# Filling the slots in 128 pieces, and nine part rows per lane by one repeated-source DMA

## The chip, the cores and the metric

The kernel runs on one NeuronCore of one Trainium2 chip. The metric is device time in microseconds (us) of one execution. Engines are called as in the profile: PE (matrix multiplies; PEld its weight loads), DVE, ACT, POOL, and SP, which here only issues DMAs and waits. PEq, SPq and so on are the engines' instruction queues.

## The reference

The reference is two transformer-like layers on x of 8 sequences, 512 positions, 256 channels, each sublayer followed by a residual sum and a layer norm. What matters here is the first sublayer, a state space scan:

```
def step(h, inp):
    u_t, dt_t, B_t, C_t = inp
    dA = jnp.exp(dt_t[:, :, None] * A_mean)
    dB = dt_t[:, :, None] * B_t[:, None, :]
    h = dA * h + dB * u_t[:, :, None]
    y_t = jnp.einsum('bds,bs->bd', h, C_t)
```

h is 512 channels by 128 states for each of 8 sequences, over 512 positions. Then come a gated norm and projection, a ternary feed-forward of hidden width 1024, a second mixer with cumulative sums, and a mixture of 8 experts with the top 2 of each token.

## The kernel before

The kernel has three phases. `project_phase` computes, per sequence, the inputs of the scan and writes them to DRAM. The product v = dt * u and B are written as three bf16 parts each (`v_parts`, `b_parts`), whose sum is the float32 value; dt goes out as float32 (`dt_rows`) and, for 128 of 512 channels, as three parts (`dt_parts`).

`stream_phase` is the scan, with the dense layers of the previous chunk mixed in. Positions are cut into 8 chunks of 64. A step k is one position of one half of the batch (four sequences, called lanes), so a chunk has 128 steps. In a step:
- SP loads a decay tile (`dt_rows`, L577): the dt of four lanes and 384 channels, 6 KB, repeated over 128 partitions, 768 KB in all. A ring of RING = 4 slots holds them; the slot of step k + 4 is loaded once POOL has done step k (the wait at L575).
- ACT takes the exponential of the decay tile (L1130), and of a PSUM bank for the other 128 channels (L1135), three steps ahead.
- POOL multiplies the state h by the decay tile, in two instructions (L1384); DVE does it for the other channels (L1410).
- PE forms the outer product of v and B for each lane (`x_outer`, L729): a matmul over nine rows, all pairs of the three parts of v with the three of B. DVE adds it to h (L1420).
- PE reads y out of h with C (`contract`, L755).

The nine rows of a lane come from DRAM by SP (`row_block`, L555 to L571). A row block covers four positions, that is eight steps, and is double buffered. For each of 8 lanes and each part i of B, one DMA brings the three part rows of v (three partitions of 4 KB, L568) and one brings part i of B repeated on three partitions (of 1 KB, L570): six DMAs per lane, 48 per block. PE waits for a group of four lanes at L723 and L725, on counts made from LANE_IN. The first block is issued before anything else of the scan (L683), then the four first decay tiles (L684).

SP issues everything in the order that `body` (L663) writes out: at each step the decay tile of step k + 4; then, at k % 8 = 2, 3, 4 and 5, the rows of two lanes of the next block; then the rest. In chunks 1 to 7 the rest includes weights of the dense layers (28 loads of 512 KB per chunk, L614), whose steps come from tables such as H1_AT and DONE_AT. PE, ACT and DVE have their own written-out orders: the mixer layers, norms and gate stand in about the first 50 steps of a chunk, and the two 1024 x 1024 layers in steps 50 to 113. Chunk 0 has no mixed work; chunk 1 has no second mixer; chunks 2 to 6 are five turns of a hardware loop, whose addresses are computed in registers; chunk 7 is written out.

The slot fill writes a DRAM tensor `slots` of 24 x 512 rows of 1 KB, which the last phase gathers tokens into, with valid numbers, so that unused slots hold some. It is 16 DMAs from DRAM to DRAM of 768 KB, at k = 30 and 94 of each chunk (L672). Only the end of the phase waits for them (L709).

`expert_phase` routes the tokens and runs the experts.

Of the kernel before, what the change touches and what calls it, by code (L numbers as in the profile page):

```python
# [29 lines left out]
BATCH, SEQ, DIM = 8, 512, 256  # L30
INNER = 512
STATE = 128
# [7 lines left out]
PARTS = 3  # L40
PAIRS = PARTS * PARTS
# [14 lines left out]
JOBS = 2 * BATCH + EXPERTS  # L56
# [9 lines left out]
def hold(eng, passed):  # L66

    eng.sem_inc(passed, 1)
# [323 lines left out]
LANES = 4  # L392
HALVES = BATCH // LANES
# [4 lines left out]
CHUNKS = SEQ // CHUNK  # L398
HALF_STEPS = HALVES * CHUNK
SLOTS = GROUPS * CHUNK  # L400
STEPS = 4
ROW_BLOCKS = CHUNK // STEPS
# [52 lines left out]
def stream_phase(nc, bank, d, used):  # L455
# [9 lines left out]
    with ExitStack() as ctx:  # L465
        def sb(name, shape, dt=F32):
            return ctx.enter_context(nc.sbuf_tensor(name, shape, dt))

        def sem(name):
            used.append(nc.alloc_semaphore(name))  # L470
            return used[-1]
# [4 lines left out]
        vrow = sb("s_vrow", [P, BUFS, HALVES, STEPS * INNER], BF16)  # L476
        brow = sb("s_brow", [P, BUFS, HALVES, STEPS * STATE], BF16)
# [39 lines left out]
        in_v = [[sem(f"s_in_v{r}{f}") for f in range(HALVES)] for r in range(BUFS)]  # L517
        in_b = [[sem(f"s_in_b{r}{f}") for f in range(HALVES)] for r in range(BUFS)]
# [12 lines left out]
        filled = sem("s_filled")  # L531
# [16 lines left out]
            return sems[name + str(m)]  # L548

        block = ctx.enter_context(nc.Block())  # L550
        LANE_IN = LANES * PARTS * 16

        @block.sync
        def _(sp):
            def row_block(j, buf, lanes):  # L555

                if 0 in lanes:
                    sp.wait_ge(x_ps, (j + 1) * (GROUPS * STEPS))
                    hold(sp, sp_passed)
                    sp.wait_ge(e_ps, (j + 1) * (HALVES * STEPS))  # L560
                    hold(sp, sp_passed)
                    for hf in range(HALVES):
                        sp.dma_start(drow[32 * hf:32 * hf + PARTS, buf], d["DTD_STEPS"][hf, j]
                                     ).then_inc(in_e[buf], 16)
                for s in lanes:
                    q, hf = 32 * (s % LANES), s // LANES
                    for i in range(PARTS):
                        sp.dma_start(vrow[q + PARTS * i:q + PARTS * (i + 1), buf, hf], d["V_STEPS"][s, :, j]  # L568
                                     ).then_inc(in_v[buf][hf], 16)
                        sp.dma_start(brow[q + PARTS * i:q + PARTS * (i + 1), buf, hf],  # L570
                                     d["B_STEPS"][s, i, j].partition_broadcast(PARTS)).then_inc(in_b[buf][hf], 16)  # L571

            def dt_rows(k, slot):

                sp.wait_ge(pool_kept, 2 * k + 2)  # L575
                hold(sp, sp_passed)
                sp.dma_start(decay[:, slot].rearrange("p l d -> p (l d)"), d["DTP_HALF"][k].partition_broadcast(P)  # L577
                             ).then_inc(in_dt[slot], 16)

            def c_cols(c):  # L580
                sp.wait_ge(diag_ok, c * (2 * CHUNK // DIAG))
                hold(sp, sp_passed)
                sp.dma_start(ccol[:], d["C_CHUNK"][c]).then_inc(c_in, 16)
# [58 lines left out]
            def stored(m):  # L642
                sp.wait_ge(S("out_dma"), 16 * (m + 1))
                sp.sem_inc(S("out_ok"), 1)
# [18 lines left out]
            def body(c, m, last):  # L663
                for k in range(HALF_STEPS):
                    if not (last and k + RING >= HALF_STEPS):
                        dt_rows(c * HALF_STEPS + k + RING, k % RING)
                    j, r = (k - 2) // (HALVES * STEPS) + 1, (k - 2) % (HALVES * STEPS)
                    if k >= 2 and r < 4 and not (last and j == ROW_BLOCKS):
                        row_block(c * ROW_BLOCKS + j, j % BUFS, (2 * r, 2 * r + 1))
                    if k == 104 and not last:  # L670
                        c_cols(c + 1)
                    if k % (HALF_STEPS // 2) == 30:  # L672
                        sp.dma_start(d["SLOTS_FILL"][c * 2 + k // (HALF_STEPS // 2)], d["x_rows"]).then_inc(filled, 16)
                    if m is not None:
                        first = isinstance(m, int) and m == 0
                        mix(m, k, SHORT if first else FULL, not first)
# [4 lines left out]
            sp.dma_start(a_log[:], d["A_log"]).then_inc(w_in, 16)  # L681
            sp.dma_start(ccol[:], d["C_CHUNK"][0]).then_inc(c_in, 16)
            row_block(0, 0, range(BATCH))  # L683
            for k in range(RING):  # L684
                dt_rows(k, k)
# [4 lines left out]
            chunk_xT(0)  # L690
            chunk_x(0)
            body(0, None, False)
            body(1, 0, False)
            with sp.Fori(2, CHUNKS - 1) as c:
                body(c, c - 1, False)
# [10 lines left out]
                weights(CHUNKS, LATE[i], (end, FULL[i - WRING]))  # L706
            store(end)
            stored(end)
            sp.wait_ge(filled, 16 * 2 * CHUNKS)  # L709

        @block.tensor
        def _(pe):
# [5 lines left out]
            def x_outer(c, n):  # L718
# [3 lines left out]
                if at == 0 and g % 2 == 0:  # L722
                    pe.wait_ge(in_v[buf][hf], (c * (ROW_BLOCKS // BUFS) + t // (STEPS * BUFS) + 1) * LANE_IN)  # L723
                    hold(pe, pe_passed)
                    pe.wait_ge(in_b[buf][hf], (c * (ROW_BLOCKS // BUFS) + t // (STEPS * BUFS) + 1) * LANE_IN)  # L725
                    hold(pe, pe_passed)
# [1381 lines left out]
def block_kernel(nc, d, out):  # L2108
    with ExitStack() as ctx:
        bank = ctx.enter_context(nc.psum_tensor("bank", [P, 8, BANK], F32))  # L2110
        v = nc.dram_tensor("v_parts", (PARTS * BATCH * SEQ, INNER), BF16, kind="Internal").ap()
        b_ = nc.dram_tensor("b_parts", (PARTS * BATCH * SEQ, STATE), BF16, kind="Internal").ap()
        dtd = nc.dram_tensor("dt_parts", (PARTS * SEQ * BATCH, DCOLS), BF16, kind="Internal").ap()
        dtp = nc.dram_tensor("dt_rows", (SEQ * BATCH, PCOLS), F32, kind="Internal").ap()
        c_ = nc.dram_tensor("c_cols", (BATCH * STATE, SEQ), F32, kind="Internal").ap()
        y = nc.dram_tensor("y_scan", (BATCH * SEQ, INNER), F32, kind="Internal").ap()
        d = dict(d)
        d["V_SEQ"] = v.rearrange("(c s i p) d -> c s p i d", c=PARTS, s=BATCH, p=P)
        d["B_SEQ"] = b_.rearrange("(c s i p) d -> c s p i d", c=PARTS, s=BATCH, p=P)
        d["DTD_SEQ"] = dtd.rearrange("(c i p s) d -> c s p i d", c=PARTS, s=BATCH, p=P)  # L2120
        d["DTP_SEQ"] = dtp.rearrange("(i p s) d -> s p i d", s=BATCH, p=P)
        d["C_SEQ"] = c_.rearrange("(s p) t -> s p t", p=P)
        d["C_CHUNK"] = c_.rearrange("(s p) (n t) -> n p s t", p=P, t=CHUNK)
        d["V_STEPS"] = v.rearrange("(c s n t) d -> s c n (t d)", c=PARTS, s=BATCH, t=STEPS)
        d["B_STEPS"] = b_.rearrange("(c s n t) d -> s c n (t d)", c=PARTS, s=BATCH, t=STEPS)
        d["DTD_STEPS"] = dtd.rearrange("(c n t h l) d -> h n c t (l d)", c=PARTS, t=STEPS, h=HALVES, l=LANES)
        d["DTP_HALF"] = dtp.rearrange("(k l) d -> k (l d)", l=LANES)
        d["Y_BLK"] = y.rearrange("(s n r) d -> s n r d", s=BATCH, r=YBLK)
        d["Y_CHUNK"] = y.rearrange("(i l n t) d -> l n t i d", i=TT, l=2, t=CHUNK)
        mixed = nc.dram_tensor("mixed", (BATCH, P, TT, DIM), F32, kind="Internal").ap()  # L2130
        slots = nc.dram_tensor("slots", (JOBS * SEQ, DIM), F32, kind="Internal").ap()
        outs = nc.dram_tensor("expert_out", (RUN * SEQ, DIM), F32, kind="Internal").ap()
        d["MIXED"] = mixed
        d["SLOTS"], d["EXPERT_OUT"] = slots, outs
        d["SLOTS_FILL"] = slots.rearrange("(n r) d -> n r d", n=2 * CHUNKS)
        d["x_rows"] = d["x_tiles"].rearrange("s p i d -> (s p i) d")[0:JOBS * SEQ // (2 * CHUNKS)]
        d["SLOT_TILES"] = slots.rearrange("(j i p) d -> j p i d", i=TT, p=P)
        d["EXPERT_OUT_TILES"] = outs.rearrange("(j i p) d -> j p i d", i=TT, p=P)
        d["FC_ROWS"] = d["fc"].rearrange("e p k h -> (e p) (k h)")
        d["PJ_ROWS"] = d["pj"].rearrange("e p k h -> (e p) (k h)")  # L2140
        for phase in (project_phase, stream_phase):

            used = []
            phase(nc, bank, d, used)
            nc.clear_and_free_semaphores(used)
            nc.all_engine_barrier()  # L2146
        expert_phase(nc, bank, d, out)
# [69 lines left out]
```

## Time and profile before

| what | us |
|---|---|
| median of 3 timed runs | 6285.27 |
| lowest and highest | 6284.0, 6291.06 |
| the profiled execution, its own time | 6273.25 |
| its span, first to last instruction | 6271.6 |
| PE busy | 4955.4 (79% of the span) |
| POOL busy | 3952.3 (63%) |
| DVE busy | 3942.4 (63%) |
| ACT busy | 3262.1 (52%) |
| `s_vrow` row DMAs, L568 | 3072 of 12 KB |
| `s_brow` row DMAs, L570 | 3072 of 3 KB |
| `s_decay` DMAs, L577 | 1024 of 768 KB |
| `slots` DMAs, L673 | 16 of 768 KB |

Shares of the span are averages over three phases with different limits; the scan starts at about 372 us and ends at about 5029 us. All times in a profile are us from the span's start.

### The profile page before, as it was taken

To read this page: it belongs to the slowest core of one execution; us is meant where nothing else is said; L and a number is where in the kernel's file an instruction comes from. 1 tells how busy PE (TensorE), PEld (TensorE's weight loads), DVE (VectorE), ACT (ScalarE), POOL (GpSimd) and SP (SyncE) were. 2 spreads that over 40 slices of the span, in tenths; PEclk is the share of its full clock that TensorE was granted. 3 is DMA by queue.
4 is the path that set the end of the run, shared out by engine and by line. 5 is a ranking of instruction groups with operands and counts; after the bars stand their busy time and mean duration, and the time that the engine had idled before them with its cause. 6 is when DMAs were issued, how large, how long until landed. Compare 5 with 4: busy or idle time off the path is not lost. (4 is left out here: it accounts for less than half of the span.)

```text
span 6271.6 us, 90806 instructions
## 1 busy us (share of the span) xinstructions
PE 4955.4 (79%) x20772; PEld 1806.3 (29%) x20772; DVE 3942.4 (63%) x4493; ACT 3262.1 (52%) x3647; POOL 3952.3 (63%) x2254
## 2 busy tenths in 40 slices
PE   5458888987897788778977887788779877389993
PEld 3301112222222222222222222222222233256662
DVE  7758887777777776777767767776777731200003
ACT  4546665765665466646764666466647631011111
POOL 2369998986787678768876887688768800310004
PEclk8755568987997799779977997899779988589996
DMA  2356666764565466646654666466557721223233
GB/s 91 99 201 239 243 230 221 261 234 171 206 242 207 169 213 233 208 173 224 225 205 172 222 234 209 168 221 239 202 175 239 253 59 47 100 91 120 100 120 101
DMA packets 333813, 1155.00 MB, mean 184 GB/s; under 512 B 84448, under 2 KB 138208, under 8 KB 327136
## 3 DMA queue, kind: packets, MB, share of 16 engines
q1 hardware_dynamic: 311168, 1071.57, 48.8%
q0 software_dynamic: 13920, 69.22, 3.4%
q10 hardware_dynamic: 8192, 8.40, 0.4%
q8 instruction: 175, 2.87, 0.2%
q14 instruction: 358, 2.93, 0.1%
HBM read 1084.51 MB, written 77.07 MB: 185 GB/s over the span
## 5 line engine op out<-in xcount | busy, mean ns | idle before, releaser
L1384 POOL TENSOR_TENSOR s_h<-s_decay,s_h 128x768 f32<-128x768 f32 x2048 | 3679.7, 1832 | 1001.5 <-ACT s_decay L1130 678.2
L1420 DVE TENSOR_TENSOR s_h<-s_h,bank 128x1024 f32<-128x1024 f32 x2048 | 2484.6, 1215 | 600.2 <-POOL s_h L1384 402.2
L1130 ACT ACTIVATE s_decay<-s_decay,s_a_neg 128x1536 f32<-128x1536 f32 x1024 | 1606.1, 1568 | 358.4 <-DMA s_decay<-dt_rows 357.3
L729 PE MATMUL bank<-s_vrow,s_brow 9*128 9x512 bf16 x4096 | 925.7, 449 | 732.6 <-DVE s_h L1420 619.1
L755 PE MATMUL bank<-s_h,s_cdiag 128*32 128x512 f32 x8192 | 1345.9, 735 | 17.6 <-ACT s_y L1143 17.6
L1135 ACT ACTIVATE bank<-bank,s_a_neg 128x512 f32<-128x512 f32 x1024 | 673.6, 658 | 1001.1 <-PE bank L743 994.8
L729 PEld LDWEIGHTS bank<-s_vrow,s_brow 9*128 9x128 bf16 x4096 | 216.1, 93 | 2554.5 <-issue 2553.4
L1410 DVE TENSOR_TENSOR s_h<-bank,s_h 128x512 f32<-128x512 f32 x1024 | 698.5, 682 | 35.1 <-ACT bank L1135 34.5
L876 PE MATMUL bank<-m_mb,m_w 128*128 128x512 f32 x1024 | 535.8, 653 | 31.3 <-ACT m_ma L1196 26.8
L862 PE MATMUL bank<-m_ma,m_w 128*128 128x512 f32 x1024 | 528.0, 645 | 9.7 <-ACT m_mb L1191 9.6
L743 PE MATMUL bank<-s_drow,s_unit 3*128 3x512 bf16 x1024 | 456.8, 447 | 69.5 <-DMA s_drow<-dt_parts 48.7
L1826 POOL DMA_INDIRECT e_pj<-in_pj,e_rows x23 | 21.6, 939 | 555.1 <-PE bank L1856 554.5
L1957 ACT ACTIVATE e_hid<-bank 128x512 f32<-128x512 f32 x184 | 109.9, 597 | 495.2 <-PE bank L1856 495.1
L1856 PE MATMUL bank<-e_cT,e_fc 128*128 128x512 f32 x736 | 321.8, 595 | 2.0 <-DVE e_cT L2065 2.0
L1856 PE MATMUL bank<-e_pj,e_hid 128*128 128x256 f32 x1472 | 321.3, 379 | 0.0
L1856 PEld LDWEIGHTS bank<-e_pj,e_hid 128*128 128x128 f32 x1472 | 278.0, 190 | 36.9
L2065 DVE COPY e_cT<-bank 128x512 f32<-128x512 f32 x24 | 16.6, 691 | 415.1 <-PE bank L1897 415.1
L755 PEld LDWEIGHTS bank<-s_h,s_cdiag 128*32 128x32 f32 x8192 | 174.9, 117 | 321.1 <-issue 310.4
L876 PEld LDWEIGHTS bank<-m_mb,m_w 128*128 128x128 f32 x1024 | 186.3, 200 | 234.9 <-issue 234.9
L862 PEld LDWEIGHTS bank<-m_ma,m_w 128*128 128x128 f32 x1024 | 183.6, 197 | 209.8 <-issue 209.7
L2071 DVE COPY e_made<-bank 128x512 f32<-128x512 f32 x46 | 31.8, 691 | 286.0 <-PE bank L1856 286.0
L1816 POOL MEMSET e_eps<- 128x1 f32 x1 | 0.1, 98 | 323.6 <-POOLq L2146 323.6
(194 smaller groups left out, 4161.1 us busy)
## 6 DMA issues: line engine op xcount, KB each, us to landing
s_decay<-dt_rows SPq DMA_DIRECT2D x1024, 768.0 KB, 4.8
m_w<-in_units SPq DMA_DIRECT2D x224, 512.0 KB, 4.0
s_vrow<-v_parts SPq DMA_DIRECT2D x3072, 12.0 KB
s_brow<-b_parts SPq DMA_DIRECT2D x3072, 3.0 KB
v_parts<-p_part SPq DMA_DIRECT2D x24, 512.0 KB, 3.0
slots<-in_x_tiles SPq DMA_DIRECT2D x16, 768.0 KB, 6.8
e_xs<-slots SPq DMA_DIRECT2D x24, 512.0 KB, 9.6
expert_out<-e_made SPq DMA_DIRECT2D x23, 512.0 KB, 9.2
```

The source lines that it names most:

```text
L729: mm = pe.matmul(bank[:, X0 + n % 2 * PAIR + b], brow[q:q + PAIRS, buf, hf, at * STATE:(at + 1) * STATE], vrow[q:q + PAIRS, buf, hf, at * ...
L743: pe.matmul(bank[:, E0 + hf], unit[q:q + PARTS], drow[q:q + PARTS, buf, t % STEPS], start=True, stop=True).then_inc(e_ps, 1)
L755: mm = pe.matmul(bank[q * 32:(q + 1) * 32, Y0], cdiag[:, hf * LANES + q, at * BLK:(at + 1) * BLK], h[:, t % 2, hf * LANES + q], start=(at ...
L862: mm = pe.matmul(bank[:, j % 4 if tail else M0], w[:, slot, k * P:(k + 1) * P], ma[:, k], start=(k == 0), stop=(k == KH - 1))
L876: mm = pe.matmul(bank[:, j % 4 if tail else M0], w[:, slot, k * P:(k + 1) * P], mb[:, k], start=(k == 0), stop=(k == KH - 1))
L1130: act.activation(decay[:, k % RING], decay[:, k % RING], ACT.Exp, scale=a_neg[:, 1:2]).then_inc(decay_ok, 1)
L1135: act.activation(bank[:, E0 + k % HALVES], bank[:, E0 + k % HALVES], ACT.Exp, scale=a_neg[:, 1:2]).then_inc(e_ok, 1)
L1384: pool.tensor_tensor(h[:, t % 2, g * PAIR:(g + 1) * PAIR, DCOLS:], decay[:, k % RING, g % 2 * PAIR:(g % 2 + 1) * PAIR], h[:, (t + 1) % 2, ...
L1410: dve.tensor_tensor(h[:, t % 2, hf * LANES:(hf + 1) * LANES, 0:DCOLS], bank[:, E0 + hf].rearrange("p (b d) -> p b d", b=LANES), h[:, (t + ...
L1420: dve.tensor_tensor(h[:, t % 2, g * PAIR:(g + 1) * PAIR], h[:, t % 2, g * PAIR:(g + 1) * PAIR], bank[:, X0 + n % 2 * PAIR:X0 + (n % 2 + 1) ...
L1856: mm = pe.matmul(dst, lhs(k), rhs(k), start=(k == 0), stop=(k == n - 1))
L1957: act.activation(hid[:, r, m], bank[:, m % 4], ACT.Gelu).then_inc(up_ok, 1)
```

## The change

Each lane's rows come by two DMAs instead of six: the nine partitions of v are one DMA whose source, three rows, is repeated three times as a whole, and the nine of B are one DMA whose source repeats each of three rows three times. The count that PE waits for becomes a third. The slot fill is cut into 128 pieces of 96 KB, one at each step with k % 8 = 0. All copies read the same kind of data and write the same bytes as before.

```diff
-        LANE_IN = LANES * PARTS * 16
+        LANE_IN = LANES * 16
...
                 for s in lanes:
                     q, hf = 32 * (s % LANES), s // LANES
-                    for i in range(PARTS):
-                        sp.dma_start(vrow[q + PARTS * i:q + PARTS * (i + 1), buf, hf], d["V_STEPS"][s, :, j]
-                                     ).then_inc(in_v[buf][hf], 16)
-                        sp.dma_start(brow[q + PARTS * i:q + PARTS * (i + 1), buf, hf],
-                                     d["B_STEPS"][s, i, j].partition_broadcast(PARTS)).then_inc(in_b[buf][hf], 16)
+                    sp.dma_start(vrow[q:q + PAIRS, buf, hf], d["V_STEPS"][s, :, j].partition_broadcast(PARTS)
+                                 ).then_inc(in_v[buf][hf], 16)
+                    sp.dma_start(brow[q:q + PAIRS, buf, hf],
+                                 d["B_STEPS"][s, :, j].unsqueeze(1).broadcast_to([PARTS, PARTS, STEPS * STATE])
+                                 ).then_inc(in_b[buf][hf], 16)
...
-                    if k % (HALF_STEPS // 2) == 30:
-                        sp.dma_start(d["SLOTS_FILL"][c * 2 + k // (HALF_STEPS // 2)], d["x_rows"]).then_inc(filled, 16)
+                    if k % (HALVES * STEPS) == 0:
+                        sp.dma_start(d["SLOTS_FILL"][c * ROW_BLOCKS + k // (HALVES * STEPS)], d["x_rows"]
+                                     ).then_inc(filled, 16)
...
-            sp.wait_ge(filled, 16 * 2 * CHUNKS)
+            sp.wait_ge(filled, 16 * ROW_BLOCKS * CHUNKS)
...
-        d["SLOTS_FILL"] = slots.rearrange("(n r) d -> n r d", n=2 * CHUNKS)
-        d["x_rows"] = d["x_tiles"].rearrange("s p i d -> (s p i) d")[0:JOBS * SEQ // (2 * CHUNKS)]
+        d["SLOTS_FILL"] = slots.rearrange("(n r) d -> n r d", n=CHUNKS * ROW_BLOCKS)
+        d["x_rows"] = d["x_tiles"].rearrange("s p i d -> (s p i) d")[0:JOBS * SEQ // (CHUNKS * ROW_BLOCKS)]
```

## Rows read from the trace of the kernel before

**Rows 1.** The page, part 5: the POOL multiply of the scan

```profile
L1384 POOL TENSOR_TENSOR s_h<-s_decay,s_h 128x768 f32<-128x768 f32 x2048 | 3679.7, 1832 | 1001.5 <-ACT s_decay L1130 678.2
```

**Rows 2.** Stretches: us, POOL busy (x), PEclk, DMA share, GB/s

```profile
578.30:835.70 257.40, 256.34 (x146) 0.50 0.67 241
...
1076.70:1361.40 284.70, 258.22 (x145) 0.95 0.74 257
...
1659.70:1975.40 315.70, 258.12 (x145) 0.89 0.65 230
...
2279.30:2593.90 314.60, 258.39 (x145) 0.90 0.65 229
...
2897.20:3210.00 312.80, 257.83 (x145) 0.90 0.65 232
3210.00:3515.00 305.00, 202.43 (x113) 0.80 0.52 182
3515.00:3828.10 313.10, 257.97 (x145) 0.89 0.66 232
...
4127.20:4442.20 315.00, 258.48 (x145) 0.88 0.65 229
4442.20:4741.50 299.30, 203.27 (x112) 0.80 0.55 191
4741.50:5028.70 287.20, 257.37 (x144) 0.93 0.69 239
```

**Rows 3.** Who waited for whom, steps 56 to 127, chunk 3

```profile
POOL s_h L1384 <- ACT s_decay L1130: 51.0, 29, 5.3
ACT s_decay L1130 <- DMA s_decay<-dt_rows: 47.3, 16, 6.8
...
PE bank L729 <- DMA s_brow<-b_parts: 19.2, 5, 4.9
```

**Rows 4.** Who waited for whom, steps 56 to 127, chunk 7

```profile
ACT s_decay L1130 <- DMA s_decay<-dt_rows: 22.3, 15, 3.9
...
PE bank L729 <- DMA s_brow<-b_parts: 3.3, 4, 1.8
```

**Rows 5.** Timeline of SP's queue in a turn of the loop: start us, us

```profile
2518.22 0.36 SPq L577 DMA_DIRECT2D s_decay<-dt_rows  x1
2518.76 0.27 SPq L568 DMA_DIRECT2D s_vrow<-v_parts  x1
...
2519.57 0.24 SPq L568 DMA_DIRECT2D s_vrow<-v_parts  x1
...
2523.86 2.08 SPq L577 DMA_DIRECT2D s_decay<-dt_rows  x3
```

**Rows 6.** Timeline of SP's queue in the last chunk

```profile
4854.79 0.30 SPq L568 DMA_DIRECT2D s_vrow<-v_parts  x1
...
4855.45 0.27 SPq L568 DMA_DIRECT2D s_vrow<-v_parts  x1
```

**Rows 7.** Timeline of POOL in the last chunk

```profile
4789.99 42.83 POOL L1384 TENSOR_TENSOR s_h<-s_decay,s_h 128x768 f32<-128x768 f32 x24 [2.88 <-ACT s_decay L1130]
...
4912.06 14.29 POOL L1384 TENSOR_TENSOR s_h<-s_decay,s_h 128x768 f32<-128x768 f32 x8 [3.97 <-ACT s_decay L1130]
```

**Rows 8.** Timeline of all engines where the scan starts

```profile
366.08 1.96 SPq L577 DMA_DIRECT2D s_decay<-dt_rows  x4
...
370.65 1.57 ACT L1130 ACTIVATE s_decay<-s_decay,s_a_neg 128x1536 f32<-128x1536 f32 x1 [16.16 <-DMA s_decay<-dt_rows]
```

**Rows 9.** The slot fill: line 673, and the page's part 6

```profile
L673 SPq DMA_DIRECT2D slots<-in_x_tiles x16: 543/646/1586, 492.0 to 4894.1; - x16
...
slots<-in_x_tiles SPq DMA_DIRECT2D x16, 768.0 KB, 6.8
```

**Rows 10.** Line 577, the decay copies (landing); the page's part 3, SP's queue

```profile
DMA to landing us min/median/max: 3.6/4.8/11.3
...
q1 hardware_dynamic: 311168, 1071.57, 48.8%
```

## The prediction

> **What bounds the kernel now.** The page first: PE is the busiest engine, but most of the span, from 372 to 5029 us, is the scan of the middle phase, so I read that phase alone, step by step. One step k advances four sequences once; there are 8 chunks of 128 steps. Each step needs two POOL multiplies (L1384). They are busy 3679.7 us and POOL sits idle 1001.5 us just before them, 678.2 us of it until ACT's exponential of the decay tile (L1130) is done [rows 1]. So POOL's own work is the floor of the scan, and the question is what makes ACT late.
>
> Next the windows. I cut each chunk at step 56. Chunk 0 has no other work mixed in and runs its last 72 steps in 257.4 us, 3.58 us per step with POOL busy 256.3 us: that is the floor. The same 72 steps take 284.7 us in chunk 1, 315.7, 314.6, 312.8, 313.1 and 315.0 us (mean 314.2) in chunks 2 to 6, and 287.2 us in chunk 7 [rows 2]. Chunks 2 to 6 are the turns of a hardware loop; chunks 1 and 7 are written out. Chunk 7 does the same mixed work in those steps as the loop turns do, less the last four decay copies. PE's clock is 0.90 there against 0.93, so neither work nor clock explains 27 us.
>
> Then who waited. In chunk 3 ACT waited 47.3 us for decay copies and PE 19.2 us for rows of v and B; POOL waited 51.0 us for ACT in the same stretch [rows 3]. In chunk 7 the two are 22.3 and 3.3 us [rows 4]. So the copies come late, and less so where the code is written out.
>
> Last, SP's queue, which issues them all. In a row step of a loop turn it issues one decay copy and six pairs of a v and a B copy. A pair takes 2519.57 - 2518.76 = 0.81 us here (most are at 0.77), and the next decay copy can go only at 2523.86 us, 5.64 us after the last [rows 5]. POOL needs 3.58. Four of eight steps are such steps, so by the fourth SP is up to 4 x 2.06 = 8.2 us behind, and a decay slot that POOL had freed stands empty. A copy then takes 4.8 us to land [rows 10]; the ring of four slots gives three steps, 10.7 us, less 1.57 us of exponential [rows 8], so some 9.1 us. 8.2 + 4.8 is over it. Written out, without the address arithmetic, a pair takes 0.66 us [rows 6], a step 0.4 + 6 x 0.66 = 4.4 us, and SP is at most some 3.3 us behind.
>
> **The row copies.** 2048 of 3072 pairs go. A row step of SP becomes one decay copy, 0.54 us [rows 5], and two pairs. No row shows a combined copy. Its bounds: as a single one now, about 0.39 us in the loop (half a pair) [rows 5], and above, three singles, 1.17 us, if its three groups cost what three copies cost. I take 0.45 us, near the single, since the decay copy, which writes 128 rows, costs just 0.36 us [rows 5]. That gives 0.54 + 4 x 0.45 = 2.3 us, under 3.58, so SP is never behind. Only above 0.76 us does it fall behind at all.
>
> What that is worth: chunks 3 and 7 differ by 66.5 - 25.6 = 40.9 us of such waits and by 27.4 us of time, 0.67 us per us of wait. All of chunk 3's waits at this rate are 44.6 us, which gives 270 us; chunk 7 comes to 287.2 - 17.2 = 270 us. I take 272 us, since some copies will still be late behind weight copies: 5 x (314.2 - 272) = 211 us, plus 15 us for chunk 7. Chunk 1 goes to about 270: 14 us. The ends are nothing and the floor of 257.4 us, 5 x 56.8 + 29.8 + 27.3 = 341 us.
>
> The first 56 steps of a loop turn are another case: 305.0 us in chunk 5, but still 299.3 us in chunk 7, where SP is prompt [rows 2]. They are held by the mixed work, in ACT's and PE's fixed order, not by copies. The gain is 0 to 5.7 us; I take 2.4 us, 12 us in five turns.
>
> At the start, the first row block's 48 copies stand ahead of the first decay copy (366.08 us), for which ACT waited 16.16 us [rows 8]. At 0.33 us [rows 6] they cost 15.8 us; 16 cost 5.3 to 7.2. Straight on the path: 8.6 to 10.5, taken as 9.5 us.
>
> PE's waits for rows count 12 copies per lane group before, 4 after; the waits stand where they stood, and nothing new queues behind them. The bytes and the order of use are the same.
>
> **The slot fill.** 112 more issues at 0.65 us [rows 9] are 73 us of SP, and its address arithmetic adds perhaps 15. They sit at k % 8 = 0, between the row bursts, where SP has a decay copy and at times a weight copy (0.54 us each of 3.58), so each is hidden; it lands by nobody's wait until the phase ends. If that cover were gone it would be up to 90 us. In return no 768 KB piece with 6.8 us to landing [rows 9] stands in the DMA engines ahead of a decay copy. The 3.97 us stall of POOL at 4912.06, 18 us after the last fill (4894.1), may be partly that, but 2.88 us at 4789.99 has no fill near it [rows 7, 9]. I count the fill as nothing, between -90 and +16.
>
> **Sum**: 211 + 15 + 14 + 12 + 9.5 = 261 us. The profiled execution took 6273.25 us, so 6012; the three timed runs have a median of 6285.27, 12 us above it, and on their scale it is 6024 us.
>
> **Rules of the Trainium skill against it.** Twelve copies at half a pair's 0.77 to 0.81 us are 4.6 to 4.9 us of SP, as long as the 4.8 us that a decay copy takes to land [rows 5, 10]. The Trainium skill ("DMA: Bandwidth & Descriptors", Issuing engines are not separate DMA queues) says that the sequencer's time to start a DMA "is usually small relative to the DMA itself"; by that rule nothing but the DMA bytes would matter here, the bytes do not change, and the sum would be near 0. This case's rows disagree with it; that outcome has (b)'s time, and its chance is within (b)'s.
>
> **Rivals.** (a) *The mixed work holds the second halves too.* Once SP is prompt, ACT with its table loads and stores, or PE, is late next. Then the loop turns reach only chunk 7's 287.2 us: 5 x 27 + 9.5 = 145 us, 6140 us. For it: stalls such as 2.88 us [rows 7]. Against it: chunk 7 still has 25.6 us of copy waits [rows 4]. Chance 0.17.
>
> (b) *The combined copy costs what three did*, or SP's time never mattered, so the change takes nothing off the path: a step stays at 0.54 + 4 x 1.17 = 5.2 us. About 6280 us. Chance 0.04.
>
> (c) *Slower: the combined copy's nine rows go down one DMA engine.* Its source begins with a repeated dimension of three. Price: SP's queue moved 1071.57 MB in 48.8% of 16 engines' span [rows 10], 21.9 GB/s per engine while busy. In eight steps an engine has a sixteenth of the decay copies, 384 KB, and about 56 KB of weights; the row copies are 8 x 45 = 360 KB. All on one: 800 KB, 37.4 us, where POOL needs 28.6. Nine such blocks are 337 us: 5 x 23 + 50 + 52 more in chunks 2 to 7 and 1, and in chunk 0, without weights, 56; the first halves of chunks 0 and 1 add some 60. Slower by 320 us with the gain at the start, 6605. It decides above 625 KB per engine, when fewer than three engines share the rows: three give 560 KB, 26.2 us. For it: the margin is thin. Against it: the copies of before also had three rows each, and chunk 1 ran with DMA share 0.74 [rows 2]. Chance 0.07. The Trainium skill (the same page, Rules for kernel authors) says that an outermost dimension of size c under 16, such as a leading repeat of c copies, confines a DMA to at most c engines; by that rule this copy has at most three, which is (c)'s question of one or three. No row shows which engines carry it.
>
> **Numbers.** The forecast has 0.72, its own range 5990 to 6070 us (268 or 276 us instead of 272, and an issue cost up to 0.76 us). Measurements tell from no change about 0.2%, 13 us. Faster: 0.72 + 0.17 = 0.89; same: (b), 0.04; slower: (c), 0.07. The range must take in the forecast's bounds and most of (a): 5965 to 6165 us; below it only a scan at the floor, above it (b) and (c).
>
> **What would show it.** SP's timeline: row steps of about 2.3 us, combined copies near 0.45 us; 1024 of each in the page. The windows: last 72 steps of chunks 2 to 6 at 265 to 280 us, first 56 within 5 us of now, chunk 7's second half near 272. Waits of ACT for decay copies under 15 us per half and PE's for rows gone. ACT's first decay at about 361 us. Wrong if SP is prompt and the second halves stay over 285 us (a), if combined issues are over 0.8 us (b), or if decay landings rise well above 8 us in the row steps (c).

## The result, and the profile after

The changed kernel has a median of 6115.19 us in four runs (6108.71 to 6129.83), beside 6287.85 us for the kernel before on the same chip: a ratio of 0.9729, 95% interval 0.971 to 0.9748. That is 173 us less, where 261 were forecast. The profiled execution took 6108.71 us. Lines of the scan have moved by one; the v copy is L567, the B copy L569.

The page of the kernel after, parts 3, 5 and 6:

```profile
q1 hardware_dynamic: 302464, 1071.53, 50.9%
...
L1385 POOL TENSOR_TENSOR s_h<-s_decay,s_h 128x768 f32<-128x768 f32 x2048 | 3683.4, 1841 | 807.6 <-ACT s_decay L1131 507.5
...
L1131 ACT ACTIVATE s_decay<-s_decay,s_a_neg 128x1536 f32<-128x1536 f32 x1024 | 1606.3, 1569 | 223.3 <-DMA s_decay<-dt_rows 222.0
...
s_decay<-dt_rows SPq DMA_DIRECT2D x1024, 768.0 KB, 5.2
```

POOL's idle time before the multiply fell from 1001.5 us [rows 1] to 807.6, and what it waited for ACT from 678.2 to 507.5. Bytes and busy times stayed; a decay copy lands a little later, 5.2 us for 4.8 [rows 10].

The windows of the kernel after, by the POOL multiply, last 72 steps of chunks 0 to 7 in order (us, POOL busy, PE clock, DMA share, GB/s):

```profile
574.00:830.20 256.20, 256.14 (x145) 0.50 0.72 243
...
1080.90:1352.90 272.00, 257.64 (x144) 0.96 0.80 268
...
1651.20:1940.50 289.30, 258.29 (x144) 0.93 0.70 249
...
2235.50:2524.30 288.80, 258.24 (x144) 0.94 0.71 249
...
3406.20:3688.90 282.70, 258.45 (x145) 0.95 0.72 254
...
4565.30:4840.50 275.20, 257.09 (x144) 0.95 0.75 250
```

Beside [rows 2]: the loop turns (chunks 2 to 6; the other two took 283.5 and 282.7 us) went from a mean of 314.2 to 285.4 us, chunk 7 from 287.2 to 275.2, chunk 1 from 284.7 to 272.0. Chunk 0 is still the floor. (The means of five are taken from unrounded times, here and below.) So the gain is where it was looked for, in the second halves, and there is less of it.

SP's timeline in a row step of a loop turn, kernel after (start us, us):

```profile
2347.56 0.38 SPq L577 DMA_DIRECT2D s_decay<-dt_rows  x1
2348.13 0.76 SPq L567 DMA_DIRECT2D s_vrow<-v_parts  x1
2349.10 0.74 SPq L569 DMA_DIRECT2D s_brow<-b_parts  x1
...
2352.07 0.37 SPq L577 DMA_DIRECT2D s_decay<-dt_rows  x1
```

This is the row to set against [rows 5]. A combined copy occupies SP for 0.74 to 0.76 us, and with the address arithmetic the next one starts 2349.10 - 2348.13 = 0.97 us later (0.93 for others in the same burst). The forecast's 0.45 us stood for that whole distance, as the single copy's 0.39 did. The row step is 2352.07 - 2347.56 = 4.51 us: shorter than 5.64, but still over POOL's 3.58. SP still falls behind in a row burst, by about half as much per step (0.93 us for 2.06).

Who waited for whom in the kernel after, last 72 steps of chunk 3, as in [rows 3] (us in total, times, longest):

```profile
ACT s_decay L1131 <- DMA s_decay<-dt_rows: 33.0, 15, 4.7
...
POOL s_h L1385 <- ACT s_decay L1131: 23.6, 19, 2.9
...
PE bank L730 <- DMA s_brow<-b_parts: 5.1, 4, 1.7
```

ACT's waits for decay copies went from 47.3 to 33.0 us, PE's for rows from 19.2 to 5.1.

The timeline of the kernel after where the scan starts:

```profile
352.49 0.90 SPq L567 DMA_DIRECT2D s_vrow<-v_parts  x1
...
364.70 1.94 SPq L577 DMA_DIRECT2D s_decay<-dt_rows  x4
...
369.25 1.57 ACT L1131 ACTIVATE s_decay<-s_decay,s_a_neg 128x1536 f32<-128x1536 f32 x1 [12.96 <-DMA s_decay<-dt_rows]
```

The kernel before, its first row copy:

```profile
350.55 0.28 SPq L568 DMA_DIRECT2D s_vrow<-v_parts  x1
```

The 16 row copies take 364.70 - 352.49 = 12.2 us; the 48 took 15.5 (from 350.55 to 366.08 [rows 8]). Here the row copies began 1.9 us later, so ACT begins only 1.4 us earlier.

### The profile page after: what moved, and what is told of

It is laid out like the page before. It is cut to its first block and busy times, and to the rows that moved or that the text cites. A ratio compares the mean times of both kernels' runs of the same rounds, so it can differ in the third digit from the quotient of the medians.

```text
span 6107.0 us, 83127 instructions
## 1 busy us (share of the span) xinstructions
PE 4849.5 (79%) x20772; PEld 1785.9 (29%) x20772; DVE 3936.6 (64%) x4493; ACT 3261.4 (53%) x3647; POOL 3955.9 (65%) x2254
## 5 line engine op out<-in xcount | busy, mean ns | idle before, releaser
L1385 POOL TENSOR_TENSOR s_h<-s_decay,s_h 128x768 f32<-128x768 f32 x2048 | 3683.4, 1841 | 807.6 <-ACT s_decay L1131 507.5
L1131 ACT ACTIVATE s_decay<-s_decay,s_a_neg 128x1536 f32<-128x1536 f32 x1024 | 1606.3, 1569 | 223.3 <-DMA s_decay<-dt_rows 222.0
L730 PE MATMUL bank<-s_vrow,s_brow 9*128 9x512 bf16 x4096 | 910.5, 442 | 672.8 <-DVE s_h L1421 636.7
L756 PE MATMUL bank<-s_h,s_cdiag 128*32 128x512 f32 x8192 | 1311.8, 718 | 21.7 <-ACT s_y L1144 21.7
L863 PE MATMUL bank<-m_ma,m_w 128*128 128x512 f32 x1024 | 514.3, 631 | 9.3 <-ACT m_mb L1192 9.3
L877 PE MATMUL bank<-m_mb,m_w 128*128 128x512 f32 x1024 | 508.5, 625 | 12.6 <-ACT m_ma L1197 10.0
```

The lines of the kernel that those rows point to most:

```text
L730: mm = pe.matmul(bank[:, X0 + n % 2 * PAIR + b], brow[q:q + PAIRS, buf, hf, at * STATE:(at + 1) * STATE], vrow[q:q + PAIRS, buf, hf, at * ...
L756: mm = pe.matmul(bank[q * 32:(q + 1) * 32, Y0], cdiag[:, hf * LANES + q, at * BLK:(at + 1) * BLK], h[:, t % 2, hf * LANES + q], start=(at ...
L863: mm = pe.matmul(bank[:, j % 4 if tail else M0], w[:, slot, k * P:(k + 1) * P], ma[:, k], start=(k == 0), stop=(k == KH - 1))
L877: mm = pe.matmul(bank[:, j % 4 if tail else M0], w[:, slot, k * P:(k + 1) * P], mb[:, k], start=(k == 0), stop=(k == KH - 1))
L1131: act.activation(decay[:, k % RING], decay[:, k % RING], ACT.Exp, scale=a_neg[:, 1:2]).then_inc(decay_ok, 1)
L1385: pool.tensor_tensor(h[:, t % 2, g * PAIR:(g + 1) * PAIR, DCOLS:], decay[:, k % RING, g % 2 * PAIR:(g % 2 + 1) * PAIR], h[:, (t + 1) % 2, ...
```

## The experiments

### Which part does it

The row copies alone. Against the changed kernel, only the fill goes back to that of before (excerpt):

```diff
-                    if k % (HALVES * STEPS) == 0:
+                    if k % (HALF_STEPS // 2) == 30:
```

> The row copies of the change with the slot fill of before (16 pieces of 768 KB). Theory (the gain is SP's issue time taken out of the row steps): the row copies carry all of it, so 6115 us within 15, against 6115 with both parts, and last 72 steps of the loop turns near 285 us. Rival (the fill's large pieces held up decay copies): without the small pieces a part of the gain is lost, 6140 us or more, and POOL stalls again by 1 to 4 us after steps 30 and 94.

Measured: 6120.6 us (6099.96 to 6133.55) beside 6277.9, ratio 0.9736 [0.9712, 0.9759]. The loop's second halves take 290.4 us on average, chunk 7's 278.3. That is the whole change within the scatter. The rival, 6140 us or more without the small pieces, did not come.

The fill alone. Against the changed kernel, the six row copies per lane come back (excerpt):

```diff
-                    sp.dma_start(vrow[q:q + PAIRS, buf, hf], d["V_STEPS"][s, :, j].partition_broadcast(PARTS)
+                    for i in range(PARTS):
+                        sp.dma_start(vrow[q + PARTS * i:q + PARTS * (i + 1), buf, hf], d["V_STEPS"][s, :, j]
...
```

> The slot fill in 128 pieces with the row copies of before. Theory: 112 more issues fall where SP has time, and the gain of small pieces is small, so 6288 us within 15. Rival 1: the small pieces are worth something, 6270 us or less. Rival 2: SP, which is late in this kernel, is made later by the 0.65 us issues, up to 90 us slower, 6300 to 6375 us.

Measured: 6253.4 us (6243.65 to 6258.91), ratio 0.9957 [0.9942, 0.9973]. Its windows, last 72 steps of chunks 3 and 7:

```profile
2276.50:2587.30 310.80, 258.63 (x144) 0.90 0.65 232
...
4720.40:5000.30 279.90, 258.19 (x144) 0.96 0.72 246
```

The fill alone is worth 24.5 us by the medians, which is the first rival and not the theory: the loop turns' second halves average 309.7 us and chunk 7's is 279.9. The two parts don't add up: with the rows combined (the run above beside the change itself, 6120.6 and 6115.19 us) no gain from the fill can be told from none. Why it helps only while SP is far behind was not tested; a guess is that a late decay copy then also meets the 768 KB piece.

### Is it SP's falling behind

If a burst is what hurts, the same copies in another order should do as much. Here each step with k % 8 < 7 gets one lane, one of them two, instead of four steps with two lanes each:

```diff
-                    j, r = (k - 2) // (HALVES * STEPS) + 1, (k - 2) % (HALVES * STEPS)
-                    if k >= 2 and r < 4 and not (last and j == ROW_BLOCKS):
-                        row_block(c * ROW_BLOCKS + j, j % BUFS, (2 * r, 2 * r + 1))
+                    j, r = k // (HALVES * STEPS) + 1, k % (HALVES * STEPS)
+                    if r < 7 and not (last and j == ROW_BLOCKS):
+                        row_block(c * ROW_BLOCKS + j, j % BUFS, ((0,), (1,), (2, 3), (4,), (5,), (6,), (7,))[r])
```

On the changed kernel:

> The changed kernel with the rows of one lane issued in each of seven of eight steps (two lanes in one of them) instead of two lanes in each of four. Same copies, same bytes. Theory (what is left of the stalls in the second halves is SP, whose row step takes 0.54 + 4 x 0.93 = 4.3 us in the loop since a combined copy costs 0.93 us instead of 0.45): a row step becomes 2.4 us, SP is never more than 1 us late, and the loop turns' last 72 steps go from 285 to about 272 us, in all about 6040 us. Rival 1 (the DMA engines are crowded, and copies land late for that): no change or a small one, 6100 to 6115 us, landing still 5.2 us. Rival 2 (the mixed work holds the steps): 6115 us.

Measured: 6052.21 us (6047.4 to 6066.73), ratio 0.9635 [0.9619, 0.9651]; second halves of the loop 278.9 us.

And with the copies and the fill of before, so that only the order differs from the kernel before:

> The kernel before with only the order changed: its single row copies, one lane (six copies) in each of seven of eight steps. Theory (not the number of copies counts but how far SP falls behind within the burst): a row step takes 0.54 + 6 x 0.39 = 2.9 us, under POOL's 3.58, so most of the gain comes without any combined copy: 6040 to 6110 us. Rival (what the change gained was the smaller number of copies, on SP or in the DMA engines): 6250 us or more.

Measured: 6122.5 us (6104.39 to 6140.42), ratio 0.9746 [0.9716, 0.9777]; second halves 291.8 us, above the 6040 to 6110 us expected but far from the rival's 6250. The order alone, without one copy less, brings what the whole change brings. Its page has for ACT's exponential:

```profile
L1130 ACT ACTIVATE s_decay<-s_decay,s_a_neg 128x1536 f32<-128x1536 f32 x1024 | 1604.9, 1567 | 82.4 <-DMA s_decay<-dt_rows 81.7
```

ACT waits 81.7 us for decay copies, far less than the 222.0 after the change, at the same time; but PE waits 44.1 us for rows (27.0 after the change). So a wait for a decay copy doesn't cost the scan a fixed share of its length: less of it need not mean less time.

### Is it the price of the combined copy

If DRAM holds the nine rows already (excerpt below, without the writes of the first phase), one copy of nine rows needs no repeat. The first phase writes each part three times for this (2 x 9 writes per sequence instead of 2 x 3):

```diff
-                    sp.dma_start(vrow[q:q + PAIRS, buf, hf], d["V_STEPS"][s, :, j].partition_broadcast(PARTS)
+                    sp.dma_start(vrow[q:q + PAIRS, buf, hf], d["V_STEPS"][s, :, j]
...
-                                 d["B_STEPS"][s, :, j].unsqueeze(1).broadcast_to([PARTS, PARTS, STEPS * STATE])
+                    sp.dma_start(brow[q:q + PAIRS, buf, hf], d["B_STEPS"][s, :, j]
```

> The changed kernel in its own order, but the first phase writes each part of v and of B three times, so that the nine rows of a lane are nine separate rows in DRAM, and each row copy has a source of two dimensions and no repeat. Theory (the combined copy is dear, 0.75 us instead of 0.25 to 0.36, for its source of three dimensions): the issue falls to about 0.3 us, a row step to 2.1 us, SP is prompt, and the result is what was forecast for the change: loop turns' last 72 steps near 272 to 278 us, in all 6040 us; the first phase may take 10 us longer for 25 MB more written. Rival (nine rows cost what they cost, three times a copy of three rows): the issue stays at 0.75 us and the time at 6115 us.

Measured: 6072.07 us (6059.15 to 6077.31) beside 6278.7, ratio 0.9664 [0.964, 0.9688]. SP's timeline in a row step of it:

```profile
2244.18 0.36 SPq L577 DMA_DIRECT2D s_decay<-dt_rows  x1
2244.72 0.28 SPq L568 DMA_DIRECT2D s_vrow<-v_parts  x1
2245.18 0.28 SPq L570 DMA_DIRECT2D s_brow<-b_parts  x1
...
2247.76 0.36 SPq L577 DMA_DIRECT2D s_decay<-dt_rows  x1
```

A copy is 0.28 us and the next starts 0.46 us after it, the price that the prediction had taken. The decay copies go 3.58 us apart: POOL's own pace. Its windows, chunks 3 and 7, and its row for ACT:

```profile
2223.40:2500.40 277.00, 257.25 (x145) 0.95 0.81 260
...
4527.40:4801.60 274.20, 257.00 (x144) 0.95 0.76 251
```

```profile
L1131 ACT ACTIVATE s_decay<-s_decay,s_a_neg 128x1536 f32<-128x1536 f32 x1024 | 1605.0, 1567 | 34.0 <-DMA s_decay<-dt_rows 33.4
```

The loop's second halves average 276.2 us, within the 272 to 278 expected, though the whole is 32 us over the expected 6040. ACT waits 33.4 us for decay copies in the whole scan. SP's lateness, from the end of the POOL multiply that frees a slot to the issue of its next copy, averages 3.7 us in the second halves of the loop before, 2.0 after the change, 1.5 with the single copies reordered, 0.9 with the combined ones reordered, 0.3 here.

Both together:

> The same with the rows of one lane in each of seven of eight steps. Theory: SP has a step of 0.54 + 2 x 0.39 = 1.3 us and is as prompt as it can be; against the spread kernel (6052 us), whose SP is still up to 3.6 us late in the step of two lanes, 0 to 20 us better in the scan, less what the first phase loses: 6030 to 6060 us. Rival (SP's lateness is all that holds the second halves above the floor of 257 us): 5950 to 5990 us.

Measured: 6075.13 us (6072.12 to 6078.83), ratio 0.9674 [0.9654, 0.9695], second halves 277.8 us, so neither the expected 6030 to 6060 us nor the rival's 5950 to 5990. Once SP is prompt the order is worth nothing, and SP's lateness isn't what holds the scan above its floor.

### What makes it dear

Two copies of nine rows each: v from three neighbouring sequences' rows, a source of three dimensions in which nothing is repeated, and B from a single row repeated nine times, a source of two. The matmuls get other data for this and do the same amount of work, so only times can be read from it.

```diff
-                    sp.dma_start(vrow[q:q + PAIRS, buf, hf], d["V_STEPS"][s, :, j].partition_broadcast(PARTS)
+                    sp.dma_start(vrow[q:q + PAIRS, buf, hf], d["V_STEPS"][min(s, 5):min(s, 5) + PARTS, :, j]
...
-                                 d["B_STEPS"][s, :, j].unsqueeze(1).broadcast_to([PARTS, PARTS, STEPS * STATE])
+                                 d["B_STEPS"][s, 0, j].partition_broadcast(PAIRS)
```

> The changed kernel with other data in the rows: v's nine rows come from a source of three dimensions without any repeat (three parts of three neighbouring sequences), B's from one row repeated nine times (two dimensions). It measures the issue alone. If three dimensions cost it: v 0.75 us, B about 0.3 us. If the repeat costs it: v about 0.3, B 0.75. If nine rows cost it: both 0.75 us.

Measured in one execution: 6046.88 us, second halves 276.5 us. The rows of the two source lines, first of the kernel after, then of this one, then of the one with nine rows in DRAM (ns min/median/max):

```profile
L567 SPq DMA_DIRECT2D s_vrow<-v_parts x1024: 700/734/1782, 352.5 to 4796.8; - x171
...
L569 SPq DMA_DIRECT2D s_brow<-b_parts x1024: 699/734/785, 353.4 to 4797.6; - x171
```

```profile
L567 SPq DMA_DIRECT2D s_vrow<-v_parts x1024: 714/762/920, 350.5 to 4733.1; - x171
...
L569 SPq DMA_DIRECT2D s_brow<-b_parts x1024: 286/307/1017, 351.5 to 4733.9; - x171
```

```profile
L568 SPq DMA_DIRECT2D s_vrow<-v_parts x1024: 272/285/1247, 358.4 to 4756.6; - x171
...
L570 SPq DMA_DIRECT2D s_brow<-b_parts x1024: 272/286/1513, 359.0 to 4757.0; - x171
```

Neither the repeat (0.307 us for nine-fold) nor the nine rows (0.285 us) is dear. What the dear kinds share is a source that walks the nine rows in two dimensions, three by three, while the destination has them as nine partitions: 0.73 to 0.76 us, at 36 KB of v and at 9 KB of B alike. A third dimension alone is not the price. The kernel after has another row copy with a source of three dimensions, `s_drow` (L563), three parts of four separate rows of 1 KB for three partitions:

```profile
L563 SPq DMA_DIRECT2D s_drow<-dt_parts x256: 245/267/577, 351.8 to 4784.0; - x128
```

It costs 0.27 us. There the source's first dimension is that of the partitions. Whether the split over partitions is what is dear, or any source whose shape differs from the destination's, no run separates. All of this is for sources in DRAM with rows of 1 and 4 KB.

### What varies by itself

Two things in the change's profile speak against it: the scan ends 188 us earlier but the whole span only 165 us, and the first 56 steps of chunk 1 took 251 us for 241. No line of the last phase is touched. So three kernels were profiled again on one chip.

> The kernel before once more, for a second profile. In the changed kernel's profile the last 100 us, where POOL's gathers run beside DVE's sums, end 24 us later after the scan than in the profile of before, though no line there is touched. Theory (that stretch varies from run to run by itself): from the scan's end to the last instruction this profile shows anything from 1243 to 1268 us, and the scan's stretches repeat within 3 us, the second halves of the loop turns at 314 us. Rival (it comes with the change): 1243 us again.

> The changed kernel once more, timed on the same chip as its order variant. 6115 us within 15, loop turns' second halves 283 to 290 us, first half of chunk 1 at 241 us if the 251 us of its first profile was chance, at 251 us if it comes with the change. Scan's end to the last instruction 1243 to 1268 us if that stretch varies by itself, 1267 us again if it comes with the change.

> The order variant of the changed kernel (one lane's rows in each of seven of eight steps) once more, beside it on one chip. If the difference seen between the two is real, 6052 us within 12, some 60 us under the changed kernel; if it was the chip or chance, less than 20 us under.

Measured: 6284.74 us in one execution of the kernel before; 6115.61 us (6112.12 to 6133.61) for the change, ratio 0.973 [0.9713, 0.9746] to 6284.81; 6070.52 us (6068.26 to 6076.49) for the spread order, ratio 0.9662 [0.9646, 0.9678]. The stretch from the end of the scan to the end of the span (us, PE, PEld, DVE, ACT and POOL busy, PE clock, DMA share, GB/s), for the kernel before in the profile of the prediction, then again, then for the kernel after:

```profile
5028.70:6271.60 1242.90, 938.50 (x3236) 600.42 (x3232) 208.32 (x556) 232.29 (x396) 168.36 (x176) 0.86 0.28 93
```

```profile
5015.10:6282.80 1267.70, 938.83 (x3236) 600.54 (x3232) 210.39 (x556) 232.31 (x396) 167.99 (x176) 0.85 0.27 91
```

```profile
4840.50:6107.00 1266.50, 938.00 (x3236) 600.30 (x3232) 210.47 (x556) 232.15 (x396) 168.15 (x176) 0.85 0.27 91
```

The kernel before had 1242.9 us in one execution and 1267.7 in the other, with the same busy times: the 24 us are its own variation. Over all twelve profiled executions the stretch is 1243 to 1269 us. The seven with both parts of the change had 1260 to 1269 (mean 1267), the other five 1243 to 1268 (mean 1255); so the change may cost some 12 us there, and that is left open. Chunk 1's first half took 243 us in the second profile of before and 244 in that of the change, and 239 to 251 over all twelve.

The second profile of the change also moved its main term: the loop's second halves are 292.5 us there, after 285.4, outside the 283 to 290 expected. In [rows 2] they are 314.2, in the second profile of before 313.5. While SP is near the edge a single profile is good to some 7 us per chunk; with SP prompt the two profiles of the spread order have 278.9 and 280.0.

The spread order on the changed kernel beats both kernels: 45 us under the change on one chip (some 60 were expected), 0.9662 of the time before. Nine rows in DRAM do as well (0.9664) at the price of more writes: the first row copy starts at 358.4 us for 352.5 after the change, some 6 us later, and the cheaper issues win that back (ACT's first decay is at 369.6 us for 369.3).

## Why the prediction was right, and what was off

The time, 6115 us, is in the stated range of 5965 to 6165 us and the sign is right. It is outside the 5990 to 6070 us that the prediction gave for its own account: the wider range was made to take in rival (a), which is not what happened, so the hit is in part luck. By the mean of two profiles of either kernel, the scan's end moved from 5021.9 to 4851.7 us, 170 us, and it comes from these places:

| term | forecast | measured, two profiles each |
|---|---|---|
| loop turns, last 72 steps, five times | 211 | 5 x (313.9 - 289.0) = 124 |
| loop turns, first 56 steps, five times | 12 | 5 x (301.5 - 297.7) = 19 |
| chunk 7, last 72 steps | 15 | 285.6 - 273.4 = 12 |
| chunk 1, last 72 steps | 14 | 284.1 - 273.4 = 11 |
| start of the scan | 9.5 | 372.1 - 371.0 = 1 |
| the rest (chunk 0, first halves of 1 and 7) | 0 | 2 |
| slot fill | 0, between -90 and +16 | 24.5 alone, nothing to be told on top of the rows |

**What bounds the scan** held: POOL's multiply, with ACT late behind decay copies that SP issues late in row bursts. The reordering with as many copies as before shows it most plainly.

**The row copies.** The step that failed is "I take 0.45 us, near the single". Taken as it was meant, with the address arithmetic, it measured 0.93 to 0.97 us, of which 0.73 to 0.76 are the issue itself; the prediction's bounds (0.39 and 1.17) held it. Its argument looked at the number of partitions written, and that is not what sets the price. By its own threshold, "Only above 0.76 us does it fall behind at all", SP still falls behind, and the loop turns stay at 289 us. The step behind it, 272 us for a prompt SP, was close: 276.2 us where the copies are cheap, 274.2 in chunk 7. Of the 87 us that the loop's term fell short, 5 x (289.0 - 276.2) = 64 go with the issue price and 5 x (276.2 - 272) = 21 are the target, set a little too low. In the time of the whole kernel the price is less, 6115 - 6072 = 43 us; with the cheap copies the first halves take 300.3 us and not 297.7, which gives back 13 us in five turns. Even with the price that the prediction had taken, the kernel would have gained 6278.7 - 6072.1 = 207 us and not 261.

**"0.67 us per us of wait"** as a rate was a lucky tool: the reordering with single copies ends at the change's time with 140 us less of ACT's waits. It was also taken between chunks that differ in more than the prediction says: chunk 7 lacks the last row block and the load of C (L583) too, beside the last four decay copies.

**The start** fell to the same misjudged price: 3.3 us of issue time gained, not 9.5, and less on the path. The lower bound of 8.6 us failed too, since it took "16 cost 5.3 to 7.2" from 0.33 and 0.45 us per copy; they took 12.2.

**The slot fill.** It hid its issues, as said. Its gain when alone, 24.5 us, is above the bound of +16. In the change it adds nothing measurable, so the zero in the sum did no harm.

**The first halves** moved 3.8 us each, inside 0 to 5.7. That they are held by the mixed work fits, and no run tested it. The 5.7 came from chunk 5, the slowest of the five; their mean before was 302.0 us, which leaves 2.6.

**Rivals.** (a) is there in small: with SP prompt the loop's halves stay 19 us above the floor. POOL still waits 14.0 us for ACT in such a half (chunk 3, nine rows in DRAM), and ACT 55.7 us for PE's banks. But it holds them at 276 us, not 287. What made the change look like (a) was SP, by the sign the prediction gave: it was not prompt. (b) is in good part true of the price and not of the time: the copy costs 0.93 to 0.97 of its 1.17, a row step 4.51 us of its 5.2. (c) didn't come: landings are at 5.2 us with a maximum of 11.9 (11.3 before), and the DMA share reaches 0.80 in chunk 1. Its threshold of 625 KB mixes two units; at its own 37.4 us for 800 KB, 28.6 us are 612 KB. The Trainium skill ("DMA: Bandwidth & Descriptors", Rules for kernel authors) has the rule that an outermost dimension of three confines a DMA to at most three engines. By the 26.2 us that the prediction worked out for three engines, that would leave the time as it is; no row shows which engines carried the copies.

The order of the issues alone, with the same DMAs, is worth 6277.9 - 6122.5 = 155 us. The Trainium skill's sentence (the same page, Issuing engines are not separate DMA queues) that the sequencer's time is usually small beside the DMA does not hold for this kernel.

The signs named ahead, row steps of 2.3 us and copies near 0.45, failed at once in SP's timeline and point to the term; the second halves' 289 us would alone have pointed to (a).

## What to carry to other kernels

Where one queue issues everything, write down its time per step and compare it with the pace of the bounding engine; what counts is the worst run of steps against the ring's slack, and spreading the issues over steps can bring as much as having fewer. Before folding DMAs into one, look at how its source walks the rows of the partitions written, and time one: here three copies of three rows cost SP 3 x 0.39 us in the loop, one that walks nine rows as three by three 0.93 or more, one that walks them in a single dimension 0.46. Profile a second time before explaining some 20 us that no changed line owns.

## What was not expected of the hardware

SP's time for a row copy followed the shape in which the source walks the nine rows, not bytes or repeats: in one dimension 0.29 to 0.31 us (three rows 0.25), as three by three 0.73 to 0.76. A source row repeated nine times was about as cheap as nine rows, and a source of three dimensions whose first is that of the partitions cost 0.27. This is no price list: the fill's copies from DRAM to DRAM took 0.65 us, at 96 and at 768 KB alike. And the last phase, whose instructions are the same in every kernel here, took anything from 1243 to 1269 us; the two profiles of the kernel before, 1243 and 1268, have equal busy times.
